# State-space block: small stages at other steps of the state loop, and GpSimd scaling a third of dt*u in 3 of 16 states

## The reference, cut to what matters

```python
h = tok(x)                          # 32 sequences; every second row of 750, as 3 segments of 128
h = h + mamba(layernorm(h))         # D = 256, D_INNER = 512, 16 states
h = h + moe(layernorm(h))           # 64 experts, top 8, capacity 256

# mamba, per sequence of L = 384
x_in, z = split(xz); x_conv = silu(conv4(x_in) + b_conv)
dt = softplus(x_conv @ W_dt.T + b_dt); Bm = x_conv @ W_B.T; Cm = x_conv @ W_C.T
for each state n:  h_n[l] = exp(dt*A_n)[l] * h_n[l-1] + (dt*u)[l] * Bm[l, n];   y += h_n * Cm[:, n]
out = (y * silu(z)) @ W_out.T
```

## Time and profile before

| | us |
|---|---|
| median of 3 runs (3594.8 to 3596.6) | 3596.08 |
| the profiled execution's own time | 3594.6 |
| its span | 3592.6 |
| busy in the span: PE / DVE / ACT / POOL | 3031.0 / 2899.8 / 2857.8 / 2103.7 |
| first scan starts, last scan ends | 83.6, 3047.4 |
| mean granted clock of TensorE | 0.951 |

### The profile page before, as it was taken

One profiled execution on the slowest core, in us unless ns is written; L12 is line 12 of the kernel. 1 busy time (PEld: TensorE's weight loads), 2 busy tenths in 40 slices (PEclk: granted clock), 3 DMA queues, 4 the chain that ended last, 5 costly groups with the idle time before them and its releaser, 6 DMA issues. The chain is left out here.

```text
span 3592.6 us, 62145 instructions
## 1 busy us (share of the span) xinstructions
PE 3031.0 (84%) x19009; PEld 2429.8 (68%) x19009; DVE 2899.8 (81%) x4756; ACT 2857.8 (80%) x5580; POOL 2103.7 (59%) x780
## 2 busy tenths in 40 slices
PE   5889888989899998989899989898989897566664
PEld 3677777777777777777777777777777776455453
DVE  3888999998999898989998989999999988544442
ACT  4999999999999999999999999998999997121110
POOL 0666556565555555555655555656555666077776
PEclk9999999999999999999999999999999999588887
DMA  2111111111111111121111111111111210267774
GB/s 89 44 47 54 55 60 60 60 60 61 51 61 50 49 58 61 60 61 60 61 60 52 60 61 60 61 60 52 52 61 60 60 51 29 66 150 148 149 150 82
DMA packets 175717, 241.42 MB, mean 67 GB/s; under 512 B 32816, under 2 KB 154128, under 8 KB 175376
## 3 DMA queue, kind: packets, MB, share of 16 engines
q1 hardware_dynamic: 150800, 199.44, 17.7%
q0 software_dynamic: 24576, 37.77, 6.3%
HBM read 176.07 MB, written 61.08 MB: 66 GB/s over the span
## 5 line engine op out<-in xcount | busy, mean ns | idle before, releaser
L349 POOL TENSOR_TENSOR hid<-hid,c_all 128x1536 f32<-128x1536 f32 x512 | 1769.0, 3455 | 1281.8 <-DVEq L567 1278.7
L572 DVE TENSOR_TENSOR_SCAN hid<-decay,hid,psB 128x1024 f32<-128x1024 f32 x512 | 1201.6, 2347 | 103.5 <-PE psB L836 61.1
L367 ACT ACTIVATE dbu_t<-dtu_t,b_t 128x512 f32<-128x512 f32 x1536 | 993.9, 712 | 186.4 <-PE psB L836 180.6
L836 PE MATMUL psB<-ident,dbu_t 128*128 128x128 f32 x6144 | 879.9, 280 | 257.3 <-DVE hid L572 245.5
L379 ACT ACTIVATE decay<-dt,a_neg 128x383 f32<-128x383 f32 x2048 | 1086.3, 606 | 0.0
L836 PEld LDWEIGHTS psB<-ident,dbu_t 128*128 128x128 f32 x6144 | 693.4, 143 | 424.8 <-DVE hid L572 342.5
L848 PE MATMUL psY<-ident,hid 128*128 128x128 f32 x6144 | 785.6, 280 | 3.5 <-POOL hid L349 3.5
L848 PEld LDWEIGHTS psY<-ident,hid 128*128 128x128 f32 x6144 | 717.3, 145 | 3.7 <-POOL hid L349 3.7
L572 DVE TENSOR_TENSOR_SCAN hid<-decay,psB 128x512 f32<-128x512 f32 x512 | 623.5, 1218 | 36.1 <-PE psB L836 14.4
L908 PE MATMUL psM<-u,w_dt 128*128 128x384 f32 x1024 | 352.0, 487 | 3.8 <-ACT soft L413 2.0
L908 PEld LDWEIGHTS psM<-u,w_dt 128*128 128x128 f32 x1024 | 184.7, 190 | 106.7 <-ACT soft L413 3.1
(11 more groups left out here) (149 smaller groups left out, 3389.7 us busy)
## 6 DMA issues: line engine op xcount, KB each, us to landing
c_all<-bc_rows_dram SPq DMA_DIRECT2D x128, 768.0 KB, 4.8
out_dram<-h SPq DMA_DIRECT2D x64, 384.0 KB, 5.4
h<-out_dram SPq DMA_DIRECT2D x32, 384.0 KB, 3.5
x_weights_dram<-normed SPq DMA_DIRECT2D x32, 384.0 KB, 2.6
xs<-in_x_dram SPq DMA_DIRECT2D x32, 256.0 KB
e_wg<-in_gate_dram SPq DMA_DIRECT2D x64, 128.0 KB, 2.8
e_wu<-in_up_dram SPq DMA_DIRECT2D x64, 128.0 KB, 3.0
e_wd<-in_down_dram SPq DMA_DIRECT2D x64, 128.0 KB, 3.4
```

Of the source, the lines that this page charges most:

```text
L349: nc.gpsimd.tensor_tensor(hid[k % 4][:, :, :], hid[k % 4][:, :, :], c_all[:, k, :].unsqueeze(1).to_broadcast([P, CH, L]), ALU.mult).then_i ...
L367: last = nc.scalar.activation(dbu_t[k % 2][:, t, :], dtu_t[q][:, t, :], ACT.Copy, scale=b_t[q][:, t, k:k + 1])
L572: nc.vector.tensor_tensor_scan(h[:, lo:hi], flat(decay[k % 4])[:, lo:hi], flat(psB)[:, lo:hi], h[:, lo - 1:lo] if j else 0.0, ALU.mult, AL ...
L836: last = nc.tensor.transpose(flat(psB)[:, i * P:(i + 1) * P], dbu_t[k % 2][:, t, c * P:(c + 1) * P], ident[:, :])
```

## The change

- At nearly every step of the bodies the small stages stand elsewhere. X0 and X1 are still at step 1 of PE, but XN1 moves in front of the second part of `turn_dbu` at step 1. On DVE the second layernorm's statistics move from step 0 to step 1, `conv(0, 1)` goes ahead of the gate, the other conv instructions all go to step 4, the routing is cut into smaller parts at steps 6 to 9 and 12, `add_block` is cut in two, with the Newton step of `norm` between the halves and the norm itself behind. On PE the scores go from step 6 to 7, AT0, AT1 and YT0 to step 11 ahead of the second part of `turn_dbu`, YT2 from 13 to 12, BT from 14 to 11.
- `SLOTTED` follows: the first bank gets BT, YT2 and LG, the second keeps AT1, YT0, YT1, DU1 and O1. X2T0 and X2T1 go to a tile of their own, `turned2`.
- States 6, 7 and 14: ACT issues 2 instead of 3 instructions in `scaled_dbu`, and POOL the third as a `tensor_tensor` behind `times_c` of three states earlier; PE waits for both.
- At the start ACT no longer waits for the weights before its first work (`negated_a` at body -1).
- `chosen_dram` is laid out by 4 groups of 16 experts: each batch is stored as runs of 96 bytes, and `count_phase` loads four transfers of 3072 bytes a partition, and is unrolled.

```diff
+POOL_PART = (6, 7, 14,)
...
+            def scaled_part(b, q, k):
+                s = NS * b + k
+                pool.wait_ge(s_bs, s)
+                pool.wait_ge(s_bt, PB * (s - 1))
+                t = NSEG - 1
+                nc.gpsimd.tensor_tensor(dbu_t[k % 2][:, t, :], dtu_t[q][:, t, :],
+                                        b_t[q][:, t, k:k + 1].to_broadcast([P, DI]), ALU.mult).then_inc(s_bp, 1)
...
+                        times_c(2 * i + q, k)
+                        if k + 3 in POOL_PART:
+                            scaled_part(2 * i + q, q, k + 3)
...
-                for t in range(NSEG):
+                for t in range(NSEG - (k in POOL_PART)):
...
-            act.wait_ge(s_w, 176)
...
+                    if isinstance(b, int) and b == -1 and k == 0:
+                        negated_a()
...
+                    if k in POOL_PART:
+                        pe.wait_ge(s_bp, len(POOL_PART) * b + POOL_PART.index(k) + 1)
...
-            sp.dma_start(chosen[:, 1:NT + 1, :].rearrange("p (b s) e -> p b (s e)", s=NSEG),
-                         ch_tab.rearrange("b p s e -> p b (s e)")).then_inc(s_ld, 16)
+            for g in range(CG):
+                sp.dma_start(chosen[:, g, 1:NT + 1, :], ch_tab[g]).then_inc(s_ld[g], 16)
```

More of the change, by code:

```diff
@@ L27 @@
 PB = len(PIECES)
+CG = 4
 TAPS = 4
@@ L194, in slot, with number, last_of @@
             return 0 if name in SLOTTED[0] else 1
[L196 to L204, removed]
-            names = SLOTTED[slot(name)]
-            earlier = sum(present(o, j) for j in range(-2, b) for o in names)
-            return earlier + sum(present(o, b) for o in names[:names.index(name) + 1])
+        def number(name, batch):
+            names = SLOTTED[slot(name)]
+            at = names.index(name)
+            ahead = [LAG[o] - LAG[name] + (i <= at) for i, o in enumerate(names)]
+            if not isinstance(batch, int):
+                return batch * len(names) + sum(ahead)
+            return sum(min(max(batch + a, 0), NB) for a in ahead)
+        def last_of(*names):
+            turns = sorted(names, key=lambda o: (-LAG[o], SLOTTED[slot(o)].index(o)))
+            return {slot(o): o for o in turns}.values()
         def each(eng, body):
@@ new lines, in body @@
+                    if k == 6:
+                        if front:
+                            biased_dt(n, 1)
+                            softplus(n, 0)
+                    if k == 8:
+                        if late:
+                            copy_turned("X2T0", o, 0)
+                    if k == 9:
+                        if front:
+                            softplus(n, 1)
+                            copy_bc(n)
+                        if late:
+                            copy_turned("X2T1", o, 1)
@@ new lines, in body @@
+                    if k == 10:
+                        if back:
+                            copy_yz(m, 0)
+                    if k == 11:
+                        if back:
+                            copy_yz(m, 2)
+                    if k == 12:
+                        if front:
+                            copy_dtu(n, r, 0)
+                    if k == 13:
+                        if front:
+                            copy_dtu(n, r, 1)
+                    if k == 15:
+                        if late:
+                            exp_logits(o)
@@ L540, in body @@
                     if of:
                         decays(*of)
[L542 to L545 removed]
+                    if k == 0:
+                        if front:
+                            copy_xin(n, 0)
+                        if late:
+                            first_rstd(o, 1)
+                        if front:
+                            copy_xin(n, 1)
@@ new lines, in body @@
+                    if back and not scans and k == 0:
+                        nc.vector.engine_nop().then_inc(s_go, 1)
+                    if k == 1:
+                        if late:
+                            second_stats(o)
+                    if k == 2:
+                        if late:
+                            newton(o, 1)
+                        if front:
+                            conv(n, 0, 1)
+                        if back:
+                            gate(m, r)
+                    if k == 4:
+                        if front:
+                            conv(n, 1, 1)
+                            conv(n, 1, 2)
+                            conv(n, 0, 2)
+                            conv(n, 1, 3)
+                            conv(n, 0, 3)
@@ L940, in project_out @@
                 if part == 0:
-                    for t in range(NSEG):
-                        copied(f"YT{t}", b)
+                    for turned_to in last_of("YT0", "YT1", "YT2"):
+                        copied(turned_to, b)
                 emptied(name, b)
@@ L1033, in _ @@
+                    if k == 14:
+                        if back:
+                            project_out(m, 0)
+                            project_out(m, 1)
+                    if k == 15:
+                        if late:
+                            route(o)
             each(pe, body)
```

597 lines of the change are left out of this document (323 added, 274 removed).

## The result

| | before | after |
|---|---|---|
| median, us | 3595.44 (4 runs) | 3509.31 (4 runs, 3503.4 to 3511.8) |
| ratio, 95% interval | | 0.976 [0.974, 0.978] |
| profiled span | 3592.6 | 3510.1 |
| first scan starts, last scan ends | 83.6, 3047.4 | 73.6, 2968.5 |

The kernel is 86 us faster. The forecast was 3462 us, a gain of 134; the range and the sign held, the size did not. By stretch the trace gives −10.0 us ahead of the first scan (forecast −11), −68.9 in the state loop (−118) and −3.6 behind it (−5). So the miss is in the loop. The −3.6 hides more than it shows: from the last scan to the first product of the count phase the changed kernel takes 50.9 us instead of 61.0, but its expert products, whose text is the same, last 413.4 us instead of 408.5. In the other kernels of this document they lasted 404.7 to 410.7 us, so the size of −3.6 is partly chance.

A forecast was written before the change was run, and what follows sets the result against it. No engine bound the kernel by its total; waits on DVE's path in the state loop did. Terms summed to −3.8 us a batch, −118 over 31 intervals, with −11 at the start and −5 in the count phase: 3462 us, range 3400 to 3545.

The forecast's parts named there:

- the third term: Turn from one batch to the next: `psB` waits at scans 15 and 0 shrink, −1.2 us a batch, bounds −1.5 and 0.
- the first rival: State loop: the ring closes fully, none of the five waits is left, −5.4 us a batch, 3412 us; chance 0.20.
- no `sum_y` of 2.7 us at the turn: Sign expected in the profile after: PE's `sum_y` at the turn of the loop no longer slowed to 2.7 us.
- POOL, "0 on path": State loop: POOL's three added multiplies a batch, 1.15 us each, cost 0 on DVE's path, bounds 0 and +0.5.
- the mechanism with 1.15 us for each of three multiplies: Rival, state loop: each of POOL's 96 multiplies holds DVE for its whole 1.15 us, +110 us, 3572; chance 0.04.
- ACT's relief "0 on the path": State loop: ACT has 3 instructions a batch less, 1.9 us, counted as 0 on DVE's path and a reserve.
- The gate, −2.0: Step 2: conv ahead of the gate and statistics before scan 1 cover DVE's wait, −2.0 us a batch, bounds −2.6 and −0.9.
- The second addition, −0.95: Output product: DVE's wait for its second addition falls from 1.05 to 0.1 us a batch, bounds −1.05 and −0.3.
- Steps 7 to 11, +0.35: Scores crowd PE's fullest steps 7 to 9, and `turn_dbu` waits for AT1 at step 11: +0.35 us a batch, bounds 0 and +1.5.
- The start, −11: Before the first scan: ACT's first copy no longer waits for the weights, −11 us, bounds −12 and −6.
- The count phase: After the state loop: load −5, final store +1, fixed addresses −1, together −5 us, bounds −14 and +4.
- half is given back: Rival: PE's crowding at steps 7 to 9 and a chain at step 11 leave −2.2 us a batch, 3512 us; chance 0.20.

The follow-up runs named there:

- experiment 1: The changed kernel with GpSimd's part undone, ACT again scaling all three thirds in all 16 states: 3494.5 us, ratio 0.9713 to the kernel before.
- 12: The changed kernel with all bodies written out, no loop in the state phase, and without GpSimd's part: 3451.4 us, ratio 0.9599 to the kernel before.
- 7: The changed kernel with the gate put ahead of the Newton step and conv at step 2: 3530.5 us, ratio 0.9811 to the kernel before.
- 8: The changed kernel with both additions of the output product in a row and the Newton step behind them: 3518.7 us, ratio 0.9786 to the kernel before.
- 10: The changed kernel with the second layernorm's norm ahead of scan 8 instead of scan 6, GpSimd's part kept: 3498.3 us, ratio 0.9728 to the kernel before.
- 11: The changed kernel with all bodies written out and the second norm ahead of scan 8: 3458.8 us, ratio 0.9624 to the kernel before.
- pool_all: The changed kernel with GpSimd making the last third in 13 states, 3 to 15, instead of three: 3689.6 us, ratio 1.0261 to the kernel before.

## Why the prediction was right in direction and too large

**The step that failed** is the third term, "behind the product / turn of the body": −1.2 us a batch, with 0.81 + 1.32 / 2 of `psB` waits to become 0.3. I read PE's 1.63 us of idling ahead of `sum_y` as work that came late and would be filled ("with PE not idle before the next body"). It is mostly the turn of the loop: a gap of 1.6 to 2.2 us occurs at every turn in both kernels, and neither of the orders run here removed it. Without a turn the kernel before idles 0.7 us there, which was work that came late, and the changed one not at all. So half of the term came true, the wait in scan 15 (0.87 us a batch gone), and the other half went the wrong way, the waits at scan 0 (+1.17). The statistics and the addition had covered part of the turn on DVE; the change took the statistics from step 0, so DVE met more of the gap. The term's weaker bound, 0, named exactly this case, and the first rival spoke of "a branch that remains"; I gave neither a price. `psB` waits fell by 1.0 us in 22 batches instead of by 26. What I said of the clock was wrong too: "no `sum_y` of 2.7 us at the turn" failed at 6 of 11, where the kernel before had 7.

**The term taken as zero** that was not: POOL, "0 on path". Its multiply took 1.06 us (1.15 forecast), but held the norm for 1.31 us a batch. In the list of rivals I had the mechanism with 1.15 us for each of three multiplies and gave it 0.04; it came at one place of three. What would show it, norm instructions longer than now, did. Its sibling, ACT's relief "0 on the path", was not zero either: experiment 1 shows some 0.7 us a batch given back without it, and 1.0 if the clock at the turns is set aside. So the two cancel in large part: without the loop, 0.17 us a batch is left (12).

**What was right.** The gate, −2.0: both waits gone, and 7 brings back the 0.5 us that conv and the Newton step cover. The second addition, −0.95: gone, and 8 brings back half of the wait. Steps 7 to 11, +0.35: a wait for `psB` of 0.2 us in scan 10, nothing worse; but 1, 10 and 11 show that this stretch is the next bound. The start, −11: −10.0. The count phase: the load −4.8 (−5), while the products, with fixed addresses and the table laid out by groups, took 1.4 us more instead of 1 less; what of the changed loop, addresses and layout costs it no run separates. ACT is busy 85.2 us a batch (84.8 expected) and POOL 3.0 us more than before (3.5).

**The sum again**, in us a batch: DVE's idle time 9.19 to 6.05 is −3.1 where −3.8 was forecast, and busy +0.7 where 0 was. That is −2.4 for −3.8. In the 22 middle batches this leaves 53 us of gain for 84. The ten at the ends gained 16 instead of 34. Eight of them gained 1.8 to 2.8 us each, like the middle, but batch 0 became 0.8 us longer and the 15 steps of the last batch 2.5 us. I had multiplied a gain of the middle by all 31 intervals.

Of the rivals, "half is given back" gave 3512 us, the measured time within 3 us, but by another mechanism (crowding at steps 7 to 9 and the chain at step 11); its time was right and its reason was not.

## What to carry to other kernels

Before a wait is counted as gain, ask whether it follows the work or the place. Here a gap of PE that occurs only where the loop turns was not filled by reordering, and taking DVE's work from beside it made it dearer. Instruction transfers in the DMA rows beside such a gap are the sign to look for. Unroll a loop of long bodies where the code allows it; here that was worth 35 us before the change and 52 after. When work is handed to GpSimd, list what stands on DVE beside it *after* GpSimd's own queue has shifted, and keep DVE's two-input SBUF instructions and `TENSOR_SCALAR` from SBUF out of that place. And when a stage is moved, look at the bodies behind the last scan too: a move that won 22 us in the loop lost 8 there.

## What the runs showed of the hardware

- A DVE instruction held by GpSimd waits for nearly the whole remainder of GpSimd's instruction, whatever its own size: 201 to 1066 ns for 128x48, 332 to 1205 for 128x192, in `pool_all`. Where DVE's began first, GpSimd's 1.04 us became 1.85.
- Not held beside GpSimd: scans with one PSUM input (1218 and 2347 ns throughout), statistics, reciprocal (1353 ns, with 0.86 us of GpSimd's part beside it in `norm8`), and a `TENSOR_SCALAR` that reads PSUM (478).
- A turn of the loop left PE idle for 1.6 to 2.2 us with two 8 KB instruction transfers at each of the gaps of the changed kernel, and, at 6 of 11 turns, at half clock for most or all of the next 12 blocks. With four batches in a turn instead of two one turn was no cheaper: PE's gap was 1.7 to 2.6 us and the mean cost 3.5 us, of five turns.
- The 128 count products took 23.4 us in every kernel with fixed addresses, no loop on PE and the table by groups, for 22.0 to 22.1 with a register, a loop and the table in one; the three were changed together.
